# A half-step transformer layer on eight cores: the sum of squares of the hidden activations moves from ScalarE (ahead of the transposes) to VectorE (behind them)

## The reference, cut to what matters

```python
def _ternary_linear(x, w):                      # weights become -1, 0, +1
    alpha = jnp.mean(jnp.abs(w))
    w_q = jnp.sign(w) * (jnp.abs(w) > 0.5 * alpha)
    rms = jnp.sqrt(jnp.sum(x * x, axis=-1, keepdims=True)) / jnp.sqrt(d)
    return jnp.einsum('bsd,fd->bsf', x / (rms + EPS), w_q)

def ffn(x, w_up, w_down):
    h = jax.nn.gelu(_ternary_linear(x, w_up), approximate=False)
    return _ternary_linear(h, w_down)           # needs sum(h*h) of each row

x = x + 0.5 * ffn(layernorm(x), w_up, w_down)
x = x + attn(layernorm(x), guidance)
x = x + 0.5 * ffn(layernorm(x), w_up, w_down)
```

## Time and profile before

| what | value |
|---|---|
| time, median of 7 runs | 7046.73 us (6949.01 to 7398.62) |
| time of the profiled execution | 6948.76 us |
| its span (slowest core, 7) | 6947.2 us |
| spans of the eight cores | 6931.9 to 6947.2 us |
| mean granted TensorE clock of each core | 0.905 to 0.907 of full speed |
| TensorE matmul busy | 5288.7 us (76%) |
| ScalarE busy | 1644.0 us (24%) |
| VectorE busy | 1493.8 us (22%) |

### The profile page before, as it was taken

One profiled execution on the slowest core, in us unless ns is written; L12 is line 12 of the kernel. 1 busy time (PEld: TensorE's weight loads), 2 busy tenths in 40 slices (PEclk: granted clock), 3 DMA queues, 4 the chain that ended last, 5 costly groups with the idle time before them and its releaser, 6 DMA issues.

```text
span 6947.2 us, 63588 instructions; the slowest of 8 cores (6931.9 to 6947.2 us)
## 1 busy us (share of the span) xinstructions
PE 5288.7 (76%) x22802; PEld 2585.2 (37%) x22802; DVE 1493.8 (22%) x3961; ACT 1644.0 (24%) x2980; POOL 21.5 (0%) x57
## 2 busy tenths in 40 slices
PE   1157788887778888787888878788887878888778
PEld 0123334333333333333333333334333333433333
DVE  3641211112121111212111121211112121121221
ACT  3442222221212222122222212222221222222111
POOL 0000000000000000000000000000000000000000
PEclk9998898999989899898989989899998989989889
DMA  6520000000000000000000000000000000000000
GB/s 195 151 67 1 1 13 1 7 7 1 13 1 13 1 7 7 0 13 1 13 1 7 7 1 13 1 13 1 7 7 1 13 1 13 1 7 7 1 7 7
DMA packets 67124, 106.85 MB, mean 15 GB/s; under 512 B 7424, under 2 KB 42240, under 8 KB 66816
## 3 DMA queue, kind: packets, MB, share of 16 engines
q1 hardware_dynamic: 62208, 86.01, 4.3%
q0 software_dynamic: 4608, 16.78, 0.6%
HBM read 85.98 MB, written 16.78 MB: 15 GB/s over the span
## 4 chain that ended last, share of the span: by engine, by line
PE 73%; DVE 10%; ACT 7%; issue 6%; DMA 2%; SPq 1%; DVEq 0%; ACTq 0%; POOL 0%; POOLq 0%
PE PT_A L654 27%; PE PT_C L670 8%; PE PT_G L670 7%; PE PT_E L670 7%; PE PT_F L670 7%; PE PT_C L819 4%; PE PT_B L856 4%; PE PT_B L604 3%; DVE gfm_h L616 3%; ACT BIGf L639 2%; PE PT_E L770 2%; PE PT_C L731 2%; PE PT_B L742 1%; DVE xr L705 1%; DMA astgD<-wdn 1%
## 5 line engine op out<-in xcount | busy, mean ns | idle before, releaser
L654 PE MATMUL PT_A<-wqdnT,gfm_h 128*128 128x512 bf16 x4096 | 990.8, 398 | 286.7 <-DVE gfm_h L616 286.7
L654 PE MATMUL PT_A<-wqdnT,gfm_l 128*128 128x512 bf16 x4096 | 925.0, 379 | 38.2
L621 DVE TENSOR_TENSOR gfm_l<-PT_B,gfm_h 128x512 bf16<-128x512 f32 x512 | 354.2, 692 | 2118.8 <-ACT gfm_h L611 1222.5
L654 PEld LDWEIGHTS PT_A<-wqdnT,gfm_h 128*128 128x128 bf16 x4096 | 407.7, 102 | 816.2 <-issue 402.0
L604 PE MATMUL PT_B<-identf,BIGf 128*128 128x128 f32 x2560 | 375.6, 295 | 350.3 <-ACT BIGf L592 341.4
L639 ACT ACTIVATE BIGf<-BIGf 128x1024 f32<-128x1024 f32 x256 | 270.0, 1055 | 1479.5 <-PE PT_A L654 1479.5
L654 PEld LDWEIGHTS PT_A<-wqdnT,gfm_l 128*128 128x128 bf16 x4096 | 382.2, 97 | 581.1 <-issue 157.2
L604 PEld LDWEIGHTS PT_B<-identf,BIGf 128*128 128x128 f32 x2560 | 328.7, 153 | 422.2 <-issue 372.9
L616 DVE CAST gfm_h<-PT_B 128x512 bf16<-128x512 f32 x256 | 177.1, 692 | 1346.2 <-ACT BIGf L639 1332.6
L670 PE MATMUL PT_C<-wqupT,xnT_h 128*128 128x512 bf16 x1024 | 312.8, 460 | 43.0 <-ACT xnT_h L611 33.5
L819 PE MATMUL PT_C<-gsT,BIGf 128*128 128x512 f32 x512 | 303.7, 760 | 0.0
(11 more groups left out here) (191 smaller groups left out, 4238.4 us busy)
## 6 DMA issues: line engine op xcount, KB each, us to landing
xr<-x SPq DMA_DIRECT2D x32, 512.0 KB, 3.7
astgU<-wup SPq DMA_DIRECT2D x64, 256.0 KB, 4.4
BIGf<-wup SPq DMA_DIRECT2D x128, 128.0 KB, 3.5
astgD<-wdn SPq DMA_DIRECT2D x64, 256.0 KB, 4.9
BIGf<-wdn SPq DMA_DIRECT2D x128, 128.0 KB, 2.6
out<-xr POOLq DMA_DIRECT2D x32, 512.0 KB, 2.9
guidN<-guid SPq DMA_DIRECT2D x16, 128.0 KB, 2.9
```

The source lines that it names most:

```text
L621: vop(lambda e, dst_h=dst_h, dst_l=dst_l, half=half: e.tensor_sub(dst_l[:, half * 512:(half + 1) * 512], PT_B[:, half * 512:(half + 1) * 512],
L654: e.matmul(PT_A[:, nh * 512:(nh + 1) * 512], src[:, i * 128:(i + 1) * 128], wqdnT[:, fg * D + nh * 512: fg * D + (nh + 1) * 512], start=(q ...
```

## The change

Two things are edited. First, `quarter_split_tr` no longer begins with a Square on ScalarE; it ends with one operation on VectorE that multiplies the slice with itself, writes the products into `er[0]` and the sum into `sg{q}`. Second, `ffn_sc` is one function again: the statistics of the next pass's even chunk are made at the head of that pass and no longer at the end of the pass before, and the columns `acol2` and `bcol2` are gone.

```diff
         def quarter_split_tr(q):
             gsrc, gbuf = gq(q)
-            sop(lambda e, gsrc=gsrc, q=q: e.activation(
-                BS[2], gsrc, AF.Square, accum_out=cols[f"sg{q}"]),
-                reads=[gbuf], writes=[bF["S2"], bF["gfm_h"], bF["gfm_l"],
-                                      bC[f"sg{q}"]])
             trsplit(gsrc, gbuf, gfm_h, gfm_l, (bF["gfm_h"], bF["gfm_l"]),
                     cast_s=(q < 2))
+            vop(lambda e, gsrc=gsrc, q=q: e.scalar_tensor_tensor(
+                er[0], gsrc, 1.0, gsrc, ALU.mult, ALU.mult,
+                accum_out=cols[f"sg{q}"]),
+                reads=[gbuf], writes=[bE[0], bC[f"sg{q}"]])
...
-    def ffn_sc_stats(c, fused=False):
-        da = "acol" if c % 2 == 0 else "acol2"
...
-    def ffn_sc_apply(c):
...
-    def ffn_sc(c, fused=False):
-        ffn_sc_stats(c, fused=fused)
-        ffn_sc_apply(c)
+    def ffn_sc(c, fused=False):
+        xa = xr[c % 4]
+        xbuf = bX[c % 4]
+        ln_stats(xa, xbuf, fused=fused, par=c % 2)
+        ln_affine_ffn()
+        sop(lambda e, xa=xa: e.activation(BS[1], xa, AF.Identity,
+                                          scale=cols["acol"], bias=cols["bcol"]),
+            reads=[xbuf, bC["acol"], bC["bcol"]], writes=[bF["S1"]])
...
-    if nch > 2:
-        ffn_sc_stats(2)
     for c in range(0, nch, 2):
         n2, n3 = c + 2 < nch, c + 3 < nch
         if n2:
-            ffn_sc_apply(c + 2)
+            ffn_sc(c + 2)
             ffn_tr(c + 2)
...
-        if c + 4 < nch:
-            ffn_sc_stats(c + 4)
```

More of the change, by code:

```diff
@@ L199, in build @@
                  "mxc", "nbc", "sumc", "invw", "tmp0", "tmp1", "tmp2",
-                 "thrp", "wacc", "acol2", "bcol2",
-                 "a2r0", "a2r1", "a2r2", "a2r3",
+                 "thrp", "wacc", "a2r0", "a2r1", "a2r2", "a2r3",
                  "b2r0", "b2r1", "b2r2", "b2r3", "eps5",
@@ L549, in ln_stats, with ln_affine_ffn @@
             reads=[bC["sqc"], bC["tmp0"]], writes=[bC["vcol"]])
-    def ln_affine_ffn(da="acol", db="bcol"):
+    def ln_affine_ffn():
         vop(lambda e: e.tensor_scalar_max(cols["tmp1"], cols["vcol"], 1e-30),
@@ L562, in ln_affine_ffn @@
             reads=[bC["tmp1"], bC["tmp2"]], writes=[bC["tmp0"]])
[L563 to L568, removed]
+        vop(lambda e: e.reciprocal(cols["acol"], cols["tmp0"]),
+            reads=[bC["tmp0"]], writes=[bC["acol"]])
+        vop(lambda e: e.scalar_tensor_tensor(cols["bcol"], cols["mcol"], -1.0,
+                                             cols["acol"], ALU.mult, ALU.mult),
+            reads=[bC["mcol"], bC["acol"]], writes=[bC["bcol"]])
     def ln_affine_plain(da, db):
@@ L580, in ln_affine_plain @@
             reads=[bC["mcol"], bC[da]], writes=[bC[db]])
-    def ffn_sc_stats(c, fused=False):
-        da = "acol" if c % 2 == 0 else "acol2"
-        db = "bcol" if c % 2 == 0 else "bcol2"
-        ln_stats(xr[c % 4], bX[c % 4], fused=fused, par=c % 2)
-        ln_affine_ffn(da, db)
-    def ffn_sc_apply(c):
-        xa = xr[c % 4]
[L590 to L594, removed]
-    def ffn_sc(c, fused=False):
-        ffn_sc_stats(c, fused=fused)
-        ffn_sc_apply(c)
+    def ffn_sc(c, fused=False):
+        xa = xr[c % 4]
+        xbuf = bX[c % 4]
[4 more added lines that the diff above has]
+            reads=[xbuf, bC["acol"], bC["bcol"]], writes=[bF["S1"]])
     def trsplit(src, srcbuf, dst_h, dst_l, dstbufs, cast_s=False):
```

## The result

The first comparison gave 0.9796 of the time before, with a 95% interval of 0.9759 to 0.9832 (median 6856.25 us over 13 runs of the changed kernel, 7047.17 us over 31 of the kernel before). On the 7046.73 us of the runs shown that ratio is 6903 us. The two profiled executions stand at 6778.01 and 6948.76 us, 0.9754. In many executions of either kernel the cores of one die (cores 0 to 3 or 4 to 7), or of both, have stretches at a lower granted clock than in these two profiles and take some per cent longer; the ratio leaves out the longest, but four of the seven executions of the changed kernel that it keeps (6818 to 6856 us) are of this kind. It therefore lies above the 0.9754. Over all executions near the lowest, the repeats further down among them, the ratio is 0.975.

A forecast was written before the change was run, and what follows sets the result against it. Time was to be had only where TensorE stands still (286.7 us before the second layer, casts held by the Square) or runs at its lower clock: 6948.8 - 101 (stall) - 65.8 (clock) = 6782 us; range 6755 to 6900.

The forecast's parts named there:

- The sum: Whole kernel: 6948.8 - 101 - 65.8 = 6782 us, 2.4% faster than the profiled execution.
- the lower end: Range's bottom: 6755 us, given as 6772 less the 15.3 us by which the eight cores' spans differ.
- my top of 6900: Range's upper end: the stall at its lower bound, 50 us gained, without the clock.
- The stall: TensorE's wait before the second layer, quarters 2 and 3: casts 0.79 us earlier, 128 times, 101 us; bounds 50 and 111.
- the row of ScalarE that I carried over: A ScalarE cast waiting for transposes alone, 0.72 us from their start, put on the pause before the second layer.
- The clock: Second-layer matmuls with `gfm_h`: no lower clock behind the shortened 1.43 us pauses, 65.8 us gained; bounds 0 and 65.8.
- the forecast of 167: Whole kernel: the gain from the stall, 101 us, and the clock, 65.8 us, together.
- The cover on VectorE: Quarter 3, ahead of the scale: added operation, 1.36 us, hidden under L705's wait of 3.08 us per call; costs nothing.
- the second case: Before the second layer: stall goes, clock doesn't come back, 6848 us; chance 0.18.
- the third: At the cast: Square not the holder, or only in part; 6899 us if the eighth transpose holds it; chance 0.10.
- the fourth: L654, quarters 2 and 3: clock falls behind every pause, 150 us more, 6998 us; chance 0.04.
- The pause at L877: TensorE pauses 31 times, 1.73 us each, without losing clock; used to expect no fall at 1.43 us.

The follow-up runs named there:

- the repeats further down: Changed kernel, unaltered, timed four more times against the kernel before; the third gave 0.9748 (0.9705 to 0.9790), the others no interval.
- the first edit alone: Kernel before with only the sum of squares moved to VectorE behind the split, statistics as before: 6768.7 us on die 0, against 6934.5 before.
- the pauses filled: Kernel before plus eight unneeded matmuls queued behind the transposes of quarters 2 and 3: 6857.7 us on that die, against 6939.0 before.
- the table: Changed kernel with 64 or 512 columns copied ahead of the first cast of quarters 2 and 3: 6773 to 6786 us and 6891 to 6901 us.

## Why the prediction was right or wrong

**The mechanism** was right at every step that could be seen: the Square held the casts, the transposes hold them now, the pause shrank, the clock stays up behind it, the statistics change nothing. One reason in it was wrong without harm: the two halves of the transposes have no semaphore each. The planner gives every engine one, which counts up, and a wait for the lower count is enough for the first half. The sum, 6782 us against the profiled execution's 6948.76, is 0.976; the profiled execution after came in at 6778.01.

**What failed is the step from the sum to the predicted time and range**, "against the profiled execution's time of 6948.76 us". I noted that this execution lay 98 us below the median of the runs shown and then wrote the predicted time and the top of the range in the microseconds of that execution alone; for chance I gave the lower end 15.3 us, the spread of cores within one execution (6772 - 15.3 is 6757; I wrote 6755), and the top nothing. The ratio measured first, 0.9796, put on that median, is 6903 us, three microseconds above my top of 6900. Had I carried the ratio over, 0.976 x 7046.73 = 6878 us would have been the time, and the same top, 6900 / 6948.76 = 0.993, would have been 6997.

The 0.9796 itself is partly chance: its interval begins at 0.9759, and the executions near the lowest over all runs stand at 0.9752. The seven executions of the changed kernel behind it spread from 6776.5 to 6856.25 us; in four of them a die, or both, had a mean clock of 0.903 to 0.913, and three are within 0.3% of the lowest. Of the kernel before, 16 of the 31 lie within 1.5% of its lowest, and 12 of these within 0.3%. Three microseconds beyond the top say little; what the range lacked is room for such executions, and the median to be set against.

**The terms of the sum.** The stall: 101 us expected, 0.79 a pause; 2.22 - 1.48 = 0.74 measured, 95 us. The missing 0.05 is between the transposes and the cast: 0.77 us on VectorE (2092.79 to 2093.56) where the row of ScalarE that I carried over had 0.72. The chain after the change shows VectorE's queue passing two waits there; which of them costs the 0.05 I didn't try.

The clock: 65.8 us at the second layer, and all of it came: 990.8 us fell to 925.4 in the first edit alone. What the prediction didn't look at are other matmuls that got faster at the same time, above all those of the attention part. On core 0 of the first edit alone:

```profile
L856 PE MATMUL PT_B<-guidN,pT 128*128 128x512 f32 x512 | 229.0, 600 | 28.5 <-ACT pT L851 28.5
```

On core 7 of the kernel before it was 247.7 us, 641 ns. From that core (6947.2 us) to this one (6772.2 us) the span fell by 175.0 us: the idle time before the second layer by 94.8, the `gfm_h` group by 65.4, L856 by 18.7, and all else rose by 3.9. So the forecast of 167 came out nearly right partly because 19 us that nobody had counted made up for 6 that the stall was short. Why L856 falls to the lower clock less often is open; with the pauses filled its counterpart got slower, 674 ns, so it doesn't simply follow the rest before the second layer.

**The cover on VectorE** held. I took 1.36 us for the operation with its read-out, 348 us in all; it is 1.30, 332 in all, and VectorE's busy time rose by 292 only, since the operation starts 0.09 us before the end of the subtraction ahead of it and its read-out 0.07 before its own end. L694 waits 100.2 us for TensorE where I expected 110, so 1.57 us of cover is left in each call. The Gelus that have to wait for it do so for some 15 us in the whole span and nobody waits for them.

**The rivals.** The clock does come back (379 against 379 ns), so the second case is out; the transposes' first half releases the cast, so the third is; and the fourth went the other way, not one more fall at a shorter pause. The pause at L877 that I used to expect this, 1.73 us, lies between the 1.61 and the 2.08 us of the table, where no pause of the second layer was tried; for the 1.48 us that came, 1.61 is the nearer row.

## What to carry to other kernels

When a junk output shares its memory with live tiles, its write waits for their readers and their writers wait for it: look at where unneeded results go before moving an operation to another engine. A pause of the matrix engine has two prices, its length and the clock behind it, and a group of matmuls behind the pause set beside an equal group without one gives the second price from two rows of one trace, for that place alone. Sum against one profiled execution, but give the forecast as a ratio and put it on the median that it will be compared with.

## What the runs showed of the hardware

Behind pauses of 1.48 and 1.61 us before the second layer the mean of its matmuls was 379 ns, as without a pause; behind 2.08 us it was higher by 16 ns and behind 2.22 us by 19, and a fall of the granted clock to 0.50 there cost 1.69 us per sixteen matmuls. Filling the pause with matmuls whose result nobody reads gave 81 us back.

A scalar_tensor_tensor over 1024 float32 values took 1215 ns from SBUF, with the same tile twice or two tiles, against 1284 ns with one source in PSUM.

In these profiles a VectorE operation that waits for nothing new started before the one ahead of it had ended: the cast began 0.14 us behind the start of a copy of 0.23 us, and 0.61 us behind that of one of 0.69.
